# Second layer: first norm two batches ahead, the mixing's rows normed on VectorE, units evicted first

## The chip, the cores and the metric

One core of one Trainium2 chip runs the whole kernel. The metric is the device time of one execution in microseconds (us); lower is better. Five engines work from queues of their own and in order: TensorE (PE in the rows, PEld its weight loads), VectorE (DVE), ScalarE (ACT), GpSimd (POOL) and SyncE (SP, which only issues DMAs here). They wait for one another on semaphores.

## The reference, cut to what matters

x has 8 batches of 1024 tokens of 128 channels, in f32. Two layers follow each other; each adds an attention part and a feed-forward part to x, both behind a modulated norm. The change touches the second layer only (`B` is 8):

```python
h = layernorm(x) * (1 + ca) + sa            # the first norm
xn = h / max(norm(h), eps) * sqrt(128) * gamma
q, kv, a = split(xn @ W_qkva.T, 3); a = sigmoid(a)
y = scan over the tokens of y[t] = a[t] * y[t-1] + kv[t]
x = x + ga * q * y
h = layernorm(x) * (1 + cb) + sb            # the second norm, for the mixing
r = sigmoid((mu_r * h + (1 - mu_r) * h_prev) @ W_r.T)   # h_prev: h of the token before
k = (mu_k * h + (1 - mu_k) * h_prev) @ W_k.T
x = x + gb * r * (relu(k) ** 2 @ W_v.T)
```

## The kernel before, in words

The first layer (attention, then an expert layer with product keys) takes the time up to about 3208 us of the span; nothing of it changes. `build_second_layer` (L1109) is the rest. x2 holds x in SBUF, 128 tokens in the partitions, 8 tiles of 128x128 a batch. A batch goes through two halves of work: scanning (first norm, products, scan, addition to x2) and mixing (second norm, products, addition, store). The program is nine rounds, b = 0 to 8, written out in order for each engine. In round b the scanning of batch b and the mixing of batch b-1 run; the first norm of batch b+1 is made ahead in the same round. Semaphores tie the engines together; no loop of hardware and no planner is involved.

Within a round of before:

- TensorE turns the units of batch b (8 transposes, two PSUM banks `ring`), turns the normed rows of batch b-1 (8 transposes, banks `obank`), makes the products a, kv, q for both halves of 512 tokens (L1492, six products), then the k and r products of the mixing (L1509 to L1517) with the turns of y between them, the v products (L1522) and the turns of their gated result. Each matmul of a 512-column product stands in the rows as two f32 matmuls.
- ScalarE evicts the turned units into xnT (L1273), evicts the turned mixing rows into `shifted` (L1289), makes the decays (sigmoid of a, L1277), norms the rows of batch b+1 in one buffer `l1_h` (L1252, 8 activations), then the gates (relu L1294, sigmoid L1296, square L1298), the sums of squares of batch b+1 (L1260), its unit rows (L1266) and last the rows of the mixing of batch b (`mix_normed`, L1282, 8 activations). So the mixing rows stand in ScalarE's queue ahead of the next round's evictions.
- VectorE makes the first moments of batch b+1 (L1338, L1343, L1345), the shift (L1348), the scans (L1374, L1376), the scale and shift of h (L1362, L1365), the additions to x2 (L1380), the second moments, the floor of the norm (L1369), the second variance, the gated products (L1394), the second shift and the last additions (L1398).
- GpSimd makes the three roots of a round, each one `pow` of 128x8 values: of the first variance (L1219), of the norm (L1223), of the second variance (L1227).
- SyncE stores a half batch of x2 as soon as its mixing is added (L1212).

In PSUM, `ring` carries turned units, then a, then turned y; `obank` the turned mixing rows, then k and r, v, and the turned result.

Of the kernel before, what the change touches and what calls it, by code (L numbers as in the profile page):

```python
# [1108 lines left out]
def build_second_layer(nc, x2, c_sb, wmod, w_qkva, w_rkv, cols, ident, half_neg, ring, obank, wide, out):  # L1109
# [4 lines left out]
    with ExitStack() as ctx:  # L1114
# [18 lines left out]
        shift = sb("l1_shift", [P, 2, TB])  # L1133
# [3 lines left out]
        h = sb("l1_h", [P, TB, D])  # L1137
# [39 lines left out]
        shift2_ready = sem("l1_shift2")  # L1177
# [37 lines left out]
        @block.gpsimd  # L1215
        def _(pool):
            def first_rstd(b):
                pool.wait_ge(var1_ready, b + 1)
                nc.gpsimd.tensor_tensor(rstd[:, 0], var[:, 0], half_neg[:, 0:TB], ALU.pow).then_inc(rstd1_ready, 1)  # L1219

            def norm_root(b):
                pool.wait_ge(floored_ready, b + 1)
                nc.gpsimd.tensor_tensor(r_norm[:], floored[:], half_neg[:, 0:TB], ALU.pow).then_inc(r_norm_ready, 1)  # L1223

            def second_rstd(b):
                pool.wait_ge(var2_ready, b + 1)
                nc.gpsimd.tensor_tensor(rstd[:, 1], var[:, 1], half_neg[:, 0:TB], ALU.pow).then_inc(rstd2_ready, 1)  # L1227

            first_rstd(0)
            norm_root(0)  # L1230
            for b in range(B):
                if b + 1 < B:
                    first_rstd(b + 1)
                    norm_root(b + 1)
                second_rstd(b)

        @block.scalar
        def _(act):
# [10 lines left out]
            def normed(b):  # L1249
                act.wait_ge(shift1_ready, b + 1)  # L1250
                for t in range(TB):
                    last = nc.scalar.activation(h[:, t], x2[:, b * TB + t], ACT.Identity, bias=shift[:, 0, t:t + 1], scale=rstd[:, 0, t:t + 1])  # L1252
                last.then_inc(normed_ready, 1)

            def sums_of_squares(b):
                act.wait_ge(h_ready, b + 1)
                if b:
                    act.wait_ge(turned, 2 * b)
                for t in range(TB):
                    last = nc.scalar.activation(unit[:, t], h[:, t], ACT.Square, accum_out=squares[:, t:t + 1])  # L1260
                last.then_inc(squares_ready, 1)

            def unit_rows(b):
                act.wait_ge(r_norm_ready, b + 1)
                for t in range(TB):
                    made = nc.scalar.activation(unit[:, t], h[:, t], ACT.Copy, scale=r_norm[:, t:t + 1])  # L1266
                    if t % 4 == 3:
                        made.then_inc(unit_ready, 1)
# [9 lines left out]

            def mix_normed(b):
                act.wait_ge(shift2_ready, b + 1)  # L1280
                for t in range(TB):
                    made = nc.scalar.activation(mixed[:, t], x2[:, b * TB + t], ACT.Identity, bias=shift[:, 1, t:t + 1], scale=rstd[:, 1, t:t + 1])  # L1282
                    if t % 4 == 3:
                        made.then_inc(mixed_ready, 1)
# [17 lines left out]
            modulation_rows()  # L1302
            sums_of_squares(0)
            unit_rows(0)
            act.wait_ge(weights_ready, 5)
            for b in range(B + 1):
                scanning, mixing, ahead = b < B, b > 0, b + 1 < B
                if scanning:
                    turned_units(b)
                if mixing:  # L1310
                    shifted_h(b - 1)
                if scanning:
                    decays(b, 0)
                if ahead:
                    normed(b + 1)
                if scanning:
                    decays(b, 1)
                if mixing:
                    gates(b - 1, 0)
                if ahead:  # L1320
# [3 lines left out]
                if ahead:  # L1324
                    unit_rows(b + 1)
                if scanning:
                    mix_normed(b)

        @block.vector
        def _(dve):  # L1330
# [16 lines left out]
            def shift_of(which):  # L1347
                return nc.vector.scalar_tensor_tensor(shift[:, which], mean_var[:, which, :, 0], -1.0, rstd[:, which], ALU.mult, ALU.mult)  # L1348

# [6 lines left out]
            def first_shift(b):  # L1356
                dve.wait_ge(rstd1_ready, b + 1)
                shift_of(0).then_inc(shift1_ready, 1)

            def scaled(b):  # L1360
                dve.wait_ge(normed_ready, b + 1)
                link(nc.vector.scalar_tensor_tensor(h[:], row(1, b), 1.0, h[:], ALU.add, ALU.mult))  # L1362

            def moved(b):
                nc.vector.tensor_tensor(h[:], h[:], row(0, b), ALU.add).then_inc(h_ready, 1)  # L1365
# [16 lines left out]
            def second_moments(b):  # L1382
                dve.wait_ge(x_scanned, 2 * b + 2)
                if b:
                    dve.wait_ge(mixed_ready, 2 * b)
                moments_of(1, b)

            def second_shift(b):
                dve.wait_ge(rstd2_ready, b + 1)
                shift_of(1).then_inc(shift2_ready, 1)  # L1390
# [34 lines left out]
            modulation_cols()  # L1425
            dve.wait_ge(rows_ready, 4)
# [3 lines left out]
            for b in range(B + 1):  # L1430
                scanning, mixing, ahead = b < B, b > 0, b + 1 < B
                if ahead:
                    first_moments(b + 1)
                    first_shift(b + 1)
                if scanning:
                    scan(b, 0)
                if ahead:
                    scaled(b + 1)
                if scanning:
                    scan(b, 1)  # L1440
                if ahead:
# [5 lines left out]
                if ahead:  # L1447
                    floor_norm(b + 1)
                if scanning:
                    variance_of(1, var2_ready)  # L1450
# [3 lines left out]
                if scanning:  # L1454
                    second_shift(b)
                if mixing:
# [4 lines left out]
        def _(pe):  # L1461
# [69 lines left out]
            for b in range(B + 1):  # L1531
                scanning, mixing = b < B, b > 0
                if scanning:
                    turn_units(b)
                if mixing:
                    turn_mixed(b - 1)
                if scanning:
                    scan_products(b, 0)
# [101 lines left out]
```

## Time and profile before

| | us |
|---|---|
| median of 3 runs (3427.01 to 3428.05) | 3428.01 |
| the profiled execution's own time | 3427.62 |
| its span, first to last instruction | 3425.8 |
| second layer in it, from about 3208 | 218 |
| TensorE busy in the span | 3052.2 (89%) |
| VectorE busy | 2475.1 (72%) |
| ScalarE busy | 1380.5 (40%) |
| GpSimd busy | 165.3 (5%) |

The shares are averages over the whole kernel, most of which is the first layer. For the second layer, rows of single stretches are read: the windows by round, the chain of waits (followed back from the last instruction, printed in order of time), and the timelines of single engines (instructions in order of time, merged where alike, with the idle time before them in brackets). A group of equal short instructions overlaps in the pipe, so their pitch (from start to start) is below the duration of one.

### The profile page before, as it was taken

How to read it: one execution, taken by the hardware profiler on the slowest of the kernel's cores; microseconds unless marked ns; L12 is line 12 of the kernel's file. 1: busy time of each engine (PE TensorE's matmuls, PEld its weight loads, DVE VectorE, ACT ScalarE, POOL GpSimd, SP SyncE). 2: the span in 40 equal slices, each digit the busy share in tenths (PEclk: the TensorE clock that was granted, in tenths of full speed). 3: DMA queues.
4: the chain of work that ended last, by engine and by line, in shares of the span. 5: the costliest groups of instructions: out<-in, count | busy, mean ns of one | idle time of the engine just before them, and what ended most of it. 6: DMA issues, size and time to landing. Idle time of an engine off the chain costs nothing. (4 is left out here: it accounts for less than half of the span.)

```text
span 3425.8 us, 82744 instructions
## 1 busy us (share of the span) xinstructions
PE 3052.2 (89%) x32384; PEld 2451.8 (72%) x32384; DVE 2475.1 (72%) x8595; ACT 1380.5 (40%) x2532; POOL 165.3 (5%) x147
## 2 busy tenths in 40 slices
PE   5999999999999999999999965787888788877688
PEld 2888888888888888888888863555565555555443
DVE  4566665756766756756656556999999999999465
ACT  1544455544455544445544511222222222222476
POOL 0000000000000000000000000000000000000121
PEclk9999999999999999999999985767666766676699
DMA  1000000000000000000000011000000000000000
GB/s 67 1 1 7 1 1 8 1 1 8 1 1 8 1 1 7 1 2 7 1 7 1 1 48 59 0 0 0 0 0 0 0 0 0 0 0 1 1 22 28
DMA packets 7559, 25.35 MB, mean 7 GB/s; under 512 B 1472, under 2 KB 1984, under 8 KB 6976
## 3 DMA queue, kind: packets, MB, share of 16 engines
q1 hardware_dynamic: 7360, 22.57, 1.7%
q8 instruction: 140, 2.29, 0.3%
q14 instruction: 59, 0.48, 0.0%
HBM read 14.18 MB, written 8.39 MB: 7 GB/s over the span
## 5 line engine op out<-in xcount | busy, mean ns | idle before, releaser
L605 PEld LDWEIGHTS obank<-v_one,probs 128*128 128x128 f32 x8192 | 1069.2, 190 | 91.2 <-issue 2.3
L605 PE MATMUL obank<-v_one,probs 128*128 128x129 f32 x8192 | 1078.6, 274 | 0.0
L352 ACT ACTIVATE probs<-bank 128x512 f32<-128x512 f32 x1024 | 583.8, 597 | 747.3 <-PE bank L593 450.8
L442 DVE TENSOR_REDUCE maxes<-ring 128x1 f32<-128x512 f32 x1024 | 660.0, 687 | 128.4 <-PE ring L573 105.4
L592 PE MATMUL bank<-q_hh,k_hl 128*128 128x512 f32 x1024 | 505.3, 493 | 1.7 <-issue 1.5
L593 PE MATMUL bank<-q_lm,k_h 65*128 65x512 f32 x1024 | 406.5, 397 | 0.0
L455 DVE RECIPROCAL recip<-obank 128x1 f32<-128x1 f32 x512 | 83.9, 164 | 415.0 <-PE obank L605 401.1
L573 PE MATMUL ring<-k_hl,q_hh 128*128 128x512 f32 x1024 | 338.3, 410 | 10.5 <-DVE k_hl L434 6.0
L973 DVE TENSOR_TENSOR low_hot<-ids,low_iota 128x16384 f16<-128x16384 f16 x32 | 278.2, 8692 | 14.7 <-ACT ids L873 13.3
L573 PEld LDWEIGHTS ring<-k_hl,q_hh 128*128 128x128 f32 x1024 | 191.6, 191 | 83.4 <-DVE k_hl L434 25.7
L1048 PE MATMUL bank<-value_hot,low_hot 64*128 64x8 f16 x16384 | 216.8, 163 | 22.2 <-issue 15.3
L1048 PEld LDWEIGHTS bank<-value_hot,low_hot 64*128 64x128 f16 x16384 | 213.3, 96 | 27.1 <-issue 16.1
L592 PEld LDWEIGHTS bank<-q_hh,k_hl 128*128 128x128 f32 x1024 | 194.0, 189 | 19.8 <-issue 19.6
L593 PEld LDWEIGHTS bank<-q_lm,k_h 65*128 65x128 f32 x1024 | 196.7, 192 | 14.4 <-issue 13.9
L1029 PE MATMUL bank<-pk_hT,downT 128*128 128x256 f32 x512 | 187.8, 545 | 13.5 <-DVE z L995 13.5
L433 DVE TENSOR_TENSOR q_lm<-ring,q_hh 64x512 fp32r<-64x512 f32 x128 | 87.4, 682 | 147.1 <-ACT q_hh L330 147.1
L1029 PEld LDWEIGHTS bank<-pk_hT,downT 128*128 128x128 f32 x512 | 144.0, 289 | 56.4 <-DVE z L995 24.5
L1064 PE MATMUL ring<-up_gated,z 128*128 128x128 f32 x1024 | 169.9, 337 | 0.0
L460 DVE SCALAR_TENSOR_TENSOR acc<-obank,recip,acc 128x128 f32<-128x128 f32 x448 | 157.2, 351 | 15.9
L1064 PEld LDWEIGHTS ring<-up_gated,z 128*128 128x128 f32 x1024 | 167.0, 255 | 0.0
L928 DVE FIND_INDEX8 top_i<-top,sims 128x8 uint16<-128x32 f32 x1024 | 165.4, 184 | 0.0
L1062 PE MATMUL ring<-x,ident_sb 128*128 (+1 forms) x128 | 37.7, 388 | 136.7 <-DVE parts L979 135.3
(211 smaller groups left out, 3539.0 us busy)
## 6 DMA issues: line engine op xcount, KB each, us to landing
xt<-in_x SPq DMA_DIRECT2D x8, 512.0 KB, 8.7
out_x<-xt SPq DMA_DIRECT2D x8, 512.0 KB, 2.6
x<-out_x SPq DMA_DIRECT2D x1, 4096.0 KB, 12.0
out_x<-x SPq DMA_DIRECT2D x16, 256.0 KB, 2.1
pk_wq<-in_w_q SPq DMA_DIRECT2D x1, 1024.0 KB, 4.8
pk_wqT<-in_w_qT SPq DMA_DIRECT2D x1, 1024.0 KB, 6.8
wmod_sb<-in_wmod SPq DMA_DIRECT2D x2, 384.0 KB, 12.5
w_qk_sb<-in_w_qk SPq DMA_DIRECT2D x1, 512.0 KB, 4.4
```

The costliest lines, as they stand in the source:

```text
L352: nc.scalar.activation(probs[:, half, i, :], st[s % 4], ACT.Exp).then_inc(st_free[s % 4], 1)
L442: nc.vector.tensor_reduce(maxes[:, i, k:k + 1], ring[bank_of(at)][:], AX.X, ALU.max).then_inc(rows_maxed, 1)
L460: out = nc.vector.scalar_tensor_tensor(acc[:, tile, :], o[:, 0:D], recip[:, tile:tile + 1], acc[:, tile, :], ALU.mult, ALU.add)
L573: give(at, nc.tensor.matmul(bank[:], q_hh[s][:, i * P:(i + 1) * P], k_hl[s][:, k * HALF:(k + 1) * HALF], start=True, stop=True))
L592: nc.tensor.matmul(st[s % 4], k_hl[w][:, keys], q_hh[w][:, queries], start=True, stop=False)
L593: nc.tensor.matmul(st[s % 4], k_h1[w][:, keys], q_lm[w][:, queries], start=False, stop=True).then_inc(st_full[s % 4], 1)
L605: mm = nc.tensor.matmul(obank[j % 2][:, 0:D + 1], probs[:, half, m, cols], v_one[h % 2][:, m, :], start=(m == 0), stop=(m == TB - 1))
L928: nc.vector.max_index(top_i[:, s, q * H + h, :], top[:, s, q * H + h, :], sims[:, q, s, h, :])
L973: nc.vector.tensor_tensor(low_hot[:].rearrange("p t (m j) -> p t m j", j=2), spread(ids[:, 0], 2, P // 2), spread(low_iota[:].rearrange("p ...
L1029: mm = nc.tensor.matmul(wide[k][:, e * 2 * P:(e + 1) * 2 * P], downT[:, col:col + P], hT[:], start=True, stop=True)
L1048: mm = nc.tensor.matmul(wide[q][:, 8 * t:8 * t + 8], low_hot[rows, t, :], value_hot[rows, t, part, :], start=(part == 0), stop=(part == 1))
L1064: mm = nc.tensor.matmul(turn_bank[:, q * D:(q + 1) * D], z[:, e, q, :], up_gated[:, e, :], start=False, stop=(e == 7))
```

## The change

One norm buffer becomes two, and the first norm runs two batches ahead: moments, root, shift and normed rows of batch b+2 are made in round b, where those of b+1 were; before the loop, batches 0 and 1 are both normed. The scale, shift, sums of squares and unit rows of batch b+1 stay in round b. The rows of the mixing move from ScalarE (end of round b) to VectorE (start of round b+1) as 8 `tensor_scalar` instructions, (x - mean) * rstd, reading mean and rstd directly, so the second shift goes. In a round, ScalarE evicts both halves of the units first, then the first decay, then the turned mixing rows; TensorE puts the first half's products ahead of the turns of the mixing rows. On VectorE the scale and shift of h follow both scans, and the second variance stands ahead of the floor of the norm.

```diff
--- before.py
+++ after.py
-        shift = sb("l1_shift", [P, 2, TB])
+        shift = sb("l1_shift", [P, TB])
...
-        h = sb("l1_h", [P, TB, D])
+        h = [sb(f"l1_h{i}", [P, TB, D]) for i in range(2)]
...
@@ -1227,10 +1226,12 @@
                 nc.gpsimd.tensor_tensor(rstd[:, 1], var[:, 1], half_neg[:, 0:TB], ALU.pow).then_inc(rstd2_ready, 1)
 
             first_rstd(0)
+            first_rstd(1)
             norm_root(0)
             for b in range(B):
+                if b + 2 < B:
+                    first_rstd(b + 2)
                 if b + 1 < B:
-                    first_rstd(b + 1)
                     norm_root(b + 1)
                 second_rstd(b)
 
...
             def normed(b):
                 act.wait_ge(shift1_ready, b + 1)
                 for t in range(TB):
-                    last = nc.scalar.activation(h[:, t], x2[:, b * TB + t], ACT.Identity, bias=shift[:, 0, t:t + 1], scale=rstd[:, 0, t:t + 1])
+                    last = nc.scalar.activation(h[b % 2][:, t], x2[:, b * TB + t], ACT.Identity, bias=shift[:, t:t + 1], scale=rstd[:, 0, t:t + 1])
                 last.then_inc(normed_ready, 1)
...
-
-            def mix_normed(b):
-                act.wait_ge(shift2_ready, b + 1)
-                for t in range(TB):
-                    made = nc.scalar.activation(mixed[:, t], x2[:, b * TB + t], ACT.Identity, bias=shift[:, 1, t:t + 1], scale=rstd[:, 1, t:t + 1])
-                    if t % 4 == 3:
-                        made.then_inc(mixed_ready, 1)
...
@@ -1300,31 +1294,29 @@
             modulation()
             normed(0)
             modulation_rows()
+            normed(1)
             sums_of_squares(0)
             unit_rows(0)
             act.wait_ge(weights_ready, 5)
             for b in range(B + 1):
-                scanning, mixing, ahead = b < B, b > 0, b + 1 < B
+                scanning, mixing = b < B, b > 0
                 if scanning:
                     turned_units(b)
+                    decays(b, 0)
                 if mixing:
                     shifted_h(b - 1)
                 if scanning:
-                    decays(b, 0)
-                if ahead:
-                    normed(b + 1)
-                if scanning:
                     decays(b, 1)
+                if b + 2 < B:
+                    normed(b + 2)
                 if mixing:
                     gates(b - 1, 0)
-                if ahead:
+                if b + 1 < B:
                     sums_of_squares(b + 1)
                 if mixing:
                     gates(b - 1, 1)
-                if ahead:
+                if b + 1 < B:
                     unit_rows(b + 1)
-                if scanning:
-                    mix_normed(b)
...
-            def shift_of(which):
-                return nc.vector.scalar_tensor_tensor(shift[:, which], mean_var[:, which, :, 0], -1.0, rstd[:, which], ALU.mult, ALU.mult)
-
...
             def first_shift(b):
                 dve.wait_ge(rstd1_ready, b + 1)
-                shift_of(0).then_inc(shift1_ready, 1)
+                nc.vector.scalar_tensor_tensor(shift[:], mean_var[:, 0, :, 0], -1.0, rstd[:, 0], ALU.mult, ALU.mult).then_inc(shift1_ready, 1)
...
                 dve.wait_ge(x_scanned, 2 * b + 2)
+                moments_of(1, b)
+
+            def mix_normed(b):
+                dve.wait_ge(rstd2_ready, b + 1)
                 if b:
-                    dve.wait_ge(mixed_ready, 2 * b)
-                moments_of(1, b)
-
-            def second_shift(b):
-                dve.wait_ge(rstd2_ready, b + 1)
-                shift_of(1).then_inc(shift2_ready, 1)
+                    dve.wait_ge(mix_turned, 2 * b)
+                for t in range(TB):
+                    made = nc.vector.tensor_scalar(mixed[:, t], x2[:, b * TB + t], mean_var[:, 1, t, 0:1], rstd[:, 1, t:t + 1], ALU.subtract, ALU.mult)
+                    if t % 4 == 3:
+                        made.then_inc(mixed_ready, 1)
...
@@ -1423,37 +1415,37 @@
             weights()
             first_shift(0)
             modulation_cols()
+            first_moments(1)
+            first_shift(1)
             dve.wait_ge(rows_ready, 4)
             scaled(0)
             moved(0)
             floor_norm(0)
             for b in range(B + 1):
-                scanning, mixing, ahead = b < B, b > 0, b + 1 < B
-                if ahead:
-                    first_moments(b + 1)
-                    first_shift(b + 1)
+                scanning, mixing = b < B, b > 0
+                if mixing:
+                    mix_normed(b - 1)
+                if b + 2 < B:
+                    first_moments(b + 2)
                 if scanning:
                     scan(b, 0)
-                if ahead:
-                    scaled(b + 1)
+                if b + 2 < B:
+                    first_shift(b + 2)
                 if scanning:
                     scan(b, 1)
-                if ahead:
+                if b + 1 < B:
+                    scaled(b + 1)
                     moved(b + 1)
                 if scanning:
                     add_scanned(b, 0)
                     add_scanned(b, 1)
                     second_moments(b)
-                if ahead:
+                    variance_of(1, var2_ready)
+                if b + 1 < B:
                     floor_norm(b + 1)
-                if scanning:
-                    variance_of(1, var2_ready)
                 if mixing:
                     gated(b - 1, 0)
                     gated(b - 1, 1)
-                if scanning:
-                    second_shift(b)
-                if mixing:
                     add_mixed(b - 1, 0)
                     add_mixed(b - 1, 1)
...
@@ -1532,10 +1524,10 @@
                 scanning, mixing = b < B, b > 0
                 if scanning:
                     turn_units(b)
+                    scan_products(b, 0)
                 if mixing:
                     turn_mixed(b - 1)
                 if scanning:
-                    scan_products(b, 0)
                     scan_products(b, 1)
                 if mixing:
                     k_product(b - 1, 0)
```

The semaphore of the second shift goes with it, and the other users of `h` read and write `h[b % 2]`.

## Rows read from the trace of the kernel before

**Rows 1.** Windows by round: length, busy time and count per engine, granted clock (PEclk), DMA.
```profile
3224.82:3243.28 18.46, 10.57 (x28) 5.35 (x28) 10.81 (x36) 10.54 (x37) 3.31 (x3) 0.68 0.00 0
3243.28:3267.06 23.78, 21.12 (x59) 10.48 (x60) 13.83 (x47) 17.79 (x52) 4.87 (x4) 0.80 0.01 1
...
3314.35:3336.31 21.96, 18.95 (x67) 9.12 (x66) 15.47 (x50) 17.73 (x53) 4.88 (x4) 1.00 0.06 24
3336.31:3359.66 23.35, 20.32 (x67) 9.97 (x66) 15.57 (x50) 17.79 (x52) 4.87 (x4) 0.93 0.06 24
...
3383.19:3425.80 42.61, 33.06 (x108) 15.71 (x106) 15.28 (x36) 20.68 (x44) 3.21 (x2) 0.96 0.10 37
```

**Rows 2.** Chain of waits, the round from 3314.35 to 3336.31: start, us, what.
```profile
3314.35 2.45 ACT l_unit L1266 x8
3316.80 3.09 ACT l_mixed L1282 x8
...
3320.59 1.04 PE ring L1492 x2
...
3323.35 0.86 PE ring L1492 x2
...
3331.51 0.45 PE ring L1464 x4
...
3331.99 0.70 DVE x L1380
...
3334.39 0.18 DVE l_floored L1369
...
3334.64 1.65 POOL l_r_norm L1223
```

**Rows 3.** Timeline of TensorE: turned units, v product, next products; end of round 7.
```profile
3316.86 0.66 PE L1464 MATMUL ring<-ident_sb,l_unit 128*128 128x128 f32 x4 [0.51 <-ACT l_unit L1266]
...
3334.97 1.10 PE L1522 MATMUL obank<-kact,w_rkv 128*128 128x512 f32 x2 [0.41 <-ACT kact L1298]
...
3342.79 1.91 PE L1492 MATMUL ring<-xnT,w_qkva 128*128 128x512 f32 x2
...
3405.50 1.10 PE L1522 MATMUL obank<-kact,w_rkv 128*128 128x512 f32 x2 [0.44 <-ACT kact L1298]
...
3411.63 1.12 PE L1509 MATMUL obank<-shifted,w_now 128*128 128x512 f32 x2
```

**Rows 4.** Timeline of ScalarE: opening, a full round, the last mixing rows.
```profile
3212.70 3.19 ACT L1252 ACTIVATE l_h<-x,l_shift,l_rstd 128x128 f32<-128x128 f32 x8 [1.66 <-DVE l_shift L1348]
...
3220.42 0.31 ACT L1260 ACTIVATE l_unit<-l_h 128x128 f32<-128x128 f32 x1 [2.61 <-DVE l_h L1365]
...
3227.43 0.69 ACT L1273 ACTIVATE xnT<-ring,l_gamma 128x512 f32<-128x512 f32 x1 [0.17 <-PE ring L1464]
...
3319.79 1.24 ACT L1273 ACTIVATE xnT<-ring,l_gamma 128x512 f32<-128x512 f32 x2
...
3407.72 3.19 ACT L1282 ACTIVATE l_mixed<-x,l_shift,l_rstd 128x128 f32<-128x128 f32 x8 [2.37 <-DVE l_shift L1348]
```

**Rows 5.** Timeline of VectorE: opening, round 0, one full round.
```profile
3217.90 1.23 DVE L1362 SCALAR_TENSOR_TENSOR l_h<-l_mod_rows,l_h 128x1024 f32<-128x1024 f32 x1 [4.09 <-ACT l_mod_rows L1247]
...
3238.36 1.28 DVE L1380 TENSOR_TENSOR x<-x,ring 128x512 f32<-128x512 f32 x2
...
3312.51 0.64 DVE L1343 BATCH_NORM_AGGREGATE l_mean_var<-l_moments 128x2 f32<-128x6 f32 x8
3313.18 0.17 DVE L1345 TENSOR_SCALAR l_var<-l_mean_var 128x8 f32<-128x8 f32 x1
```

**Rows 6.** Timeline of VectorE: single-source operations on 128x128 tiles elsewhere.
```profile
3210.70 0.47 DVE L1404 TENSOR_SCALAR w_now<-w_rkv,cols 128x128 f32<-128x128 f32 x2
...
3134.59 0.23 DVE L963 TENSOR_SCALAR chosen_u<-chosen_u 128x128 uint32<-128x128 uint32 x1
3134.73 0.22 DVE L965 TENSOR_SCALAR chosen_u<-chosen_u 128x128 uint32<-128x128 uint32 x1
```

More of the change, by code:

```diff
@@ L1176, in build_second_layer @@
         rstd2_ready = sem("l1_rstd2")
-        shift2_ready = sem("l1_shift2")
         mixed_ready = sem("l1_mixed_ready")
@@ L1259, in sums_of_squares @@
                 for t in range(TB):
-                    last = nc.scalar.activation(unit[:, t], h[:, t], ACT.Square, accum_out=squares[:, t:t + 1])
+                    last = nc.scalar.activation(unit[:, t], h[b % 2][:, t], ACT.Square, accum_out=squares[:, t:t + 1])
                 last.then_inc(squares_ready, 1)
@@ L1265, in unit_rows @@
                 for t in range(TB):
-                    made = nc.scalar.activation(unit[:, t], h[:, t], ACT.Copy, scale=r_norm[:, t:t + 1])
+                    made = nc.scalar.activation(unit[:, t], h[b % 2][:, t], ACT.Copy, scale=r_norm[:, t:t + 1])
                     if t % 4 == 3:
@@ L1357, in first_shift @@
                 dve.wait_ge(rstd1_ready, b + 1)
-                shift_of(0).then_inc(shift1_ready, 1)
+                nc.vector.scalar_tensor_tensor(shift[:], mean_var[:, 0, :, 0], -1.0, rstd[:, 0], ALU.mult, ALU.mult).then_inc(shift1_ready, 1)
             def scaled(b):
                 dve.wait_ge(normed_ready, b + 1)
-                link(nc.vector.scalar_tensor_tensor(h[:], row(1, b), 1.0, h[:], ALU.add, ALU.mult))
+                link(nc.vector.scalar_tensor_tensor(h[b % 2][:], row(1, b), 1.0, h[b % 2][:], ALU.add, ALU.mult))
             def moved(b):
-                nc.vector.tensor_tensor(h[:], h[:], row(0, b), ALU.add).then_inc(h_ready, 1)
+                nc.vector.tensor_tensor(h[b % 2][:], h[b % 2][:], row(0, b), ALU.add).then_inc(h_ready, 1)
             def floor_norm(b):
```

## The prediction

> **What bounds the kernel now.** I read the page first (TensorE busy 89% of the span), then windows cut at each start of the unit rows (L1266), since the shares are averages and the change touches only the last 218 us. A round of the second layer takes 21.96 us where TensorE has its full clock throughout (PEclk 1.00, 2.4 GHz), and 23.35 where part of it runs at 1.2 GHz (0.93) [rows 1]; three more rounds, not shown, are of the second kind, at 23.5 to 23.7. In all of them TensorE, the busiest engine, has 19 to 21 us of work, VectorE 15.5, ScalarE 17.8. So none is full, and the order of the work decides. The chain of waits shows it for the round from 3314.35 [rows 2]: ScalarE makes the unit rows (2.45), then the mixing rows (3.09); only then are the units evicted, and the products start at 3320.59, 6.24 us after the round's start. From there TensorE is busy without a gap until the second turn of y ends at 3331.96 (11.37). VectorE adds it to x2 at 3331.99, takes the second moments and floors the norm at 3334.39, GpSimd makes the root (1.65), and the next unit rows start at 3336.31 (4.32 after the addition). 6.24 + 11.37 + 0.03 + 4.32 = 21.96. The reader is to see that ScalarE's mixing rows (3.09) stand in the chain between the unit rows and their own eviction.
>
> **The part that pays: evictions at once.** The last units are turned 2.51 after the round's start and take 0.66 [rows 3], so both banks are full at 3.17. ScalarE evicts them together from 5.44 to 6.68 (3319.79, 1.24 for two) [rows 4]. With the mixing rows out of its queue it is free at 2.45, evicts the first half by 2.45 + 0.69 = 3.14, and the first product starts at 3.15. The opening batch already does this: its first eviction starts 2.61 after its unit rows [rows 4]. Gain 6.24 - 3.15 = 3.09 a round.
>
> **What comes back.** (1) The two turns of the mixing rows stood beside ScalarE's work and now stand between the first and second half's products, in TensorE's gapless stretch: 2 x 0.45 by the turn of y [rows 2] = 0.90. They hold nothing else up: with three products of 0.86 a half [rows 2], turn 0 ends near 6.2, ScalarE makes `shifted` by 7.7, and the k product is due at 9.2. (2) The second variance now stands ahead of the floor: 0.67 for the aggregation until its successor, 0.08 for the addition [rows 5] = 0.75, on the path, since it lies between moments and root. New round at full clock: 3.15 + 11.37 + 0.90 + 0.03 + 4.32 + 0.75 = 20.52, against 21.96: 1.44 less.
>
> **The mixing rows on VectorE.** 8 `tensor_scalar` of 128x128 f32 from SBUF with two scalars per partition. The nearest row, the same operation with one such scalar (w_now), takes 0.47 for two at 0.28 each, a pitch of 0.19 [rows 6]; integer ones with constants have a pitch of 0.14 [rows 6]; the upper bound is ScalarE's 3.09 / 8 = 0.39 [rows 2]. I take 0.19, 8 x 0.19 + 0.09 = 1.6 us (bounds 1.2 and 3.2). They wait for the second root, which GpSimd makes after the norm's, 1.65 after the round's start; so they stand from 1.7 to 3.3, and the moments and variance of b+2 follow (1.7 + 0.75), the first scan near 5.7. The turns want the rows at 5.8; y is wanted by TensorE at 12.6 and ready, about 2 later than the scan's start, at 7.8. VectorE's second use, scale and shift of h (2.5) after both scans, ends near 13.0, before the first addition at 13.2. Cover is thus 2.5 us for the rows; the path feels them through first shift and ScalarE's normed rows only above that (below). In the round the edit costs nothing; VectorE's work goes from 15.5 to some 17 of 20.5. Removing the second shift gives 0.08 of VectorE, off the path. The Trainium skill, "VectorE: DVE Perf Modes", the section "The perf-mode tier table", says that an f32 `tensor_scalar` from SBUF to SBUF runs at two elements a cycle. The w_now row (0.28, against 0.23 of the integer row of the same size) does not agree for the form with a scalar per partition; by the rule the rows would take about the lower bound, which moves only the tail, by 0.2.
>
> **ScalarE's new order.** Its total falls by 3.1. The normed rows of b+2 (3.19 by batch 0's [rows 4]) run from 8.2 to 11.3, after the second decay; the first relu is wanted at 11.0 and made by 11.9, the second k product wants it at 13.0 (after the turn of y). Slack 1.1. Two batches ahead nothing waits for these rows in the same round; GpSimd's first root is asked for at 5.8 and ready at 7.5, in an otherwise idle stretch. The stores on SyncE keep their order and come with the last additions.
>
> **Opening and round 0.** The second batch's norm now stands ahead of the first one's scale. Normed rows of batch 0 end at 3212.70 + 3.19 = 3215.89 [rows 4]; then moments 1.7, variance 0.75, root 1.65, shift: 3220.2, and scale and shift of h, 1.23 each, which began at 3217.90 [rows 5], end at 3222.7. ScalarE makes the second batch's rows (3.19) until 3223.4 and only then the sums of squares that began at 3220.42 [rows 4]: 2.9 later. Round 0 took 18.46 [rows 1]; in it the additions began at 3238.36, 13.5 after its start [rows 5]. With both scans ahead of scale and shift, VectorE gets h done at about 14.4 and adds then: 0.9, and the variance 0.7: 1.6 longer. Together +4.5.
>
> **Rounds 1 to 6** took 139.9 (3243.28 to 3383.19) [rows 1]. New: 6 x 20.52 = 123.1, plus 1.8 for the low clock after round 0's idle time (23.78 - 21.96, kept), = 124.9.
>
> **The clock.** A round at 0.93 costs 1.4 (1.7 in the rounds not shown) more than one at 1.00 [rows 1]; the low stretch begins with the first products. Ahead of it TensorE has, from the second v product's end (3334.97 + 1.10) to the products (3342.79), 6.7 us of nothing but turns and gaps [rows 3]. In the tail the same kind of stretch is 3406.60 to 3411.63, 5.0 us [rows 3], with no fall. After the change it is about 4.4 (19.1 to 23.6 in a round's time). So the clock should mostly hold. I put one fall of 1.7 into rounds 2 to 7 where there were five; bounds none and six (0 to 10.2). Rounds 1 to 6: 126.6 with it, a gain of 13.3.
>
> **The tail**, from 3383.19 to the end, 42.6 [rows 1] with one fall: -1.7; products earlier, turns between, -3.09 + 0.90 = -2.2 (the variance already stood there); the last mixing rows on VectorE: they started on ScalarE at 3407.72 [rows 4] and the k product at 3411.63 [rows 3], 3.9 later. On VectorE, by the same clock, 1.1 until the last additions are through, 0.85 for four rows, 0.7 turn, 0.7 `shifted` = 3.3, so -0.6. Gain 4.5, 2.8 if the clock falls.
>
> **The sum**, on the profiled execution: span 3425.8 + 4.5 - 13.3 - 4.5 = 3412.5; its own time lies 1.8 above its span, so 3414.3, and 0.4 more for the median of the runs (3428.01 against 3427.62): 3414 to 3415. I say 3414.
>
> **Rivals.** (1) The clock falls in every round, as in five of six before. The turns-only stretch of 4.4 lies close to the tail's 5.0, one instance, and round-to-round idle is still there; against it, 6.7 shrinks by a third. Five falls more, 5 x 1.7 = 8.5: 3423, within 0.2%. (2) The mixing rows on VectorE cost far more than their row. They delay moments, first shift, ScalarE's normed rows, relu, and so the second k product. It decides from 1.6 + 1.1 = 2.7 us for the eight on; at 0.65 each (5.2) each of seven rounds loses 2.5 and the tail 3.6: +21, 3435, slower. For: two scalars per partition, a form with no row; against: even ScalarE has 0.39, where the loss is 0.5 a round (+5). (3) The early start is given back: the wait moves from the unit rows to VectorE, whose queue is now the one with h, both scans and the rows in it; with only 0.7 of the 1.44 gained a round, in six rounds and the tail, 7 x 0.7 = 4.9: 3419. For: h is through 0.2 before the first addition; against: the second addition, which counts, is 2 later.
>
> **Chances.** Forecast (at most two falls, 3410 to 3418) 0.70; rival 1, 0.12; rival 3, 0.09; rival 2, 0.04; better than 3410, 0.05 (opening cheaper). A measurement of this kernel tells about 0.2%, 6.9 us, from no change, so faster means under 3421.2: 0.86; same 0.10; slower 0.04. The range runs from 3409 to 3422: below, no fall at all and half of the opening's cost hidden; above, nearly all falls.
>
> **What would show it.** In the windows of the new kernel a period of 20.5 at PEclk 1.00; in the timeline xnT evicted at 2.45 and products at 3.15 after the unit rows; in the chain no mixing rows, but the variance between moments and root; the rows on VectorE at a pitch near 0.19 from 1.7 on; the start of the first unit rows 2.9 later. It is wrong if the chain of a round passes through ScalarE's normed rows or relu, if PEclk stays at 0.93 in most rounds, or if round 0 grows by over 3.

## The result, and the profile after

The changed kernel takes 3409.73 us (median of 5 runs, 3407.49 to 3412.46) against 3427.15 (5 runs, 3426.11 to 3428.05): a ratio of 0.995, interval 0.9938 to 0.9963. Forecast were 3414, range 3409 to 3422.

The profiled execution took 3412.22 with a span of 3410.3, 15.5 less than before. Not all of it belongs to the change. The second layer's first instruction, ScalarE's table load, stands at 3206.28 here and at 3208.08 in the trace of before; over all profiles of this study, whose first 3200 us are the same code, it stands anywhere from 3205.7 to 3210.0. So I compare the layer from that table load to the end of the span: 217.7 us before, 204.0 after, 13.7 less. The predicted sum was 13.3 less.

The windows by round, as in [rows 1], cut at the starts of the unit rows (L1267 is L1266 of before):

```profile
3226.13:3246.39 20.26, 10.65 (x28) 5.38 (x28) 10.79 (x36) 10.53 (x36) 3.30 (x3) 0.67 0.00 0
3246.39:3267.73 21.34, 19.27 (x61) 9.82 (x62) 16.35 (x55) 14.94 (x44) 4.87 (x4) 0.89 0.00 1
...
3308.72:3329.22 20.50, 18.49 (x65) 9.14 (x65) 17.43 (x57) 14.82 (x44) 4.87 (x4) 1.00 0.07 26
...
3370.22:3410.30 40.08, 31.86 (x104) 15.51 (x103) 18.56 (x49) 14.64 (x28) 3.21 (x2) 0.96 0.11 40
```

Five rounds, from 3267.73 on, take 20.50 us each (the first 20.49) at PEclk 1.00, where one of before did at 21.96 and the others took 23.4 to 23.7 [rows 1]. VectorE is busy for 17.4 of them, ScalarE for 14.8; in the last of the five, which norms no further batch, for 15.1 and 11.9. The chain of waits of the same round as in [rows 2]:

```profile
3308.72 2.45 ACT l_unit L1267 x8
...
3311.88 1.04 PE ring L1484 x2
...
3314.64 0.87 PE obank L1456 x8
...
3324.15 0.70 DVE x L1369
...
3324.87 1.66 DVE l_moments L1330 x8
...
3326.55 0.65 DVE l_mean_var L1335 x8
...
3327.23 0.17 DVE l_var L1337
...
3327.55 1.65 POOL l_r_norm L1222
```

The mixing rows are gone from it. From the unit rows' start to the first product: 3.16 (6.24 in [rows 2]). The eight turns of the mixing rows stand between the products (0.87), and the second variance between moments and root (0.65 + 0.17, less the overlap). On ScalarE's timeline, opening and one round:

```profile
3218.66 3.19 ACT L1253 ACTIVATE l_h<-x,l_shift,l_rstd 128x128 f32<-128x128 f32 x8 [2.66 <-DVE l_shift L1347]
3221.76 0.29 ACT L1261 ACTIVATE l_unit<-l_h 128x128 f32<-128x128 f32 x1
...
3311.08 0.67 ACT L1274 ACTIVATE xnT<-ring,l_gamma 128x512 f32<-128x512 f32 x1
...
3316.93 3.18 ACT L1253 ACTIVATE l_h<-x,l_shift,l_rstd 128x128 f32<-128x128 f32 x8
3320.02 0.57 ACT L1288 ACTIVATE kact<-obank 128x512 f32<-128x512 f32 x1
```

The second batch's normed rows keep the sums of squares waiting until 3221.76 (batch 0 of before [rows 4]: 3220.42, in a layer that began 1.8 later), so the first unit rows start 19.85 after the layer's start where they started after 16.74. In the round the first eviction starts 2.36 after the unit rows, normed rows two batches ahead follow, and the relu is not late.

### The profile page after: what moved, and what is told of

It is laid out like the page before. It is cut to its first block and busy times, and to the rows that moved or that the text cites. A ratio compares the mean times of both kernels' runs of the same rounds, so it can differ in the third digit from the quotient of the medians.

```text
span 3410.3 us, 82730 instructions
## 1 busy us (share of the span) xinstructions
PE 3040.3 (89%) x32384; PEld 2448.4 (72%) x32384; DVE 2488.9 (73%) x8651; ACT 1355.8 (40%) x2468; POOL 165.3 (5%) x147
## 5 line engine op out<-in xcount | busy, mean ns | idle before, releaser
L973 DVE TENSOR_TENSOR low_hot<-ids,low_iota 128x16384 f16<-128x16384 f16 x32 | 278.1, 8691 | 14.1 <-ACT ids L873 13.1
L1048 PE MATMUL bank<-value_hot,low_hot 64*128 64x8 f16 x16384 | 216.9, 163 | 23.4 <-issue 16.1
L1029 PE MATMUL bank<-pk_hT,downT 128*128 128x256 f32 x512 | 188.1, 546 | 13.7 <-DVE z L995 13.5
```

Of the source, the lines that this page charges most:

```text
L973: nc.vector.tensor_tensor(low_hot[:].rearrange("p t (m j) -> p t m j", j=2), spread(ids[:, 0], 2, P // 2), spread(low_iota[:].rearrange("p ...
L1029: mm = nc.tensor.matmul(wide[k][:, e * 2 * P:(e + 1) * 2 * P], downT[:, col:col + P], hT[:], start=True, stop=True)
L1048: mm = nc.tensor.matmul(wide[q][:, 8 * t:8 * t + 8], low_hot[rows, t, :], value_hot[rows, t, part, :], start=(part == 0), stop=(part == 1))
```

## The experiments

Each is read by its layer time (from ScalarE's table load to the end of the span, in one profiled execution) and its rounds; the ratios are against the kernel before, run on the same chip. In all, the code of the first 3200 us is unchanged. Full rounds of one kernel repeat within 0.1 (the exceptions are named), but with the same instructions the tail has come out 1.6 apart and rounds 0 and 1 together 0.7 apart (both below), and most intervals of the ratios overlap. So layer times less than about 2 apart say nothing by themselves.

| kernel | layer, us | full round, us | median, us | ratio (interval) |
|---|---|---|---|---|
| before | 217.7 | 21.96 to 23.7 | 3427 to 3430 | 1 |
| the change | 204.0 | 20.50 | 3409.73 | 0.995 (0.9938 to 0.9963) |
| 1 floor ahead of the variance | 198.9 | 19.75 | 3407.01 | 0.9935 (0.9919 to 0.9952) |
| 2 mixing rows back on ScalarE | 225.5 | 23.9 to 24.2 | 3433.71 | 1.0019 (1.001 to 1.0028) |
| 3 mixing rows on VectorE alone | 204.6 | 21.54 (first 20.93) | 3413.59 | 0.9956 (0.994 to 0.9973) |
| 4 opening in another order | 201.4 | 20.50 | 3409.42 | 0.9944 (0.9928 to 0.9961) |
| 5 before, turns made thrice | 210.0 | 21.96 | 3418.81 | 0.9975 (0.9964 to 0.9985) |
| 6 extra row instructions | 207.2 | 20.84 (last 20.50) | 3415.68 | 0.9964 (0.9951 to 0.9977) |
| 7 mixing rows turned first | 204.8 | 20.74 | 3412.99 | 0.9957 (0.994 to 0.9974) |
| 8 floor ahead of the moments | 191.2 | 19.14 | 3399.63 | 0.9921 (0.9907 to 0.9935) |
| 9 gated products ahead too | 197.6 | 20.2 (last 19.23) | 3407.90 | 0.9937 (0.992 to 0.9953) |
| 10 wide row instructions | 204.9 | 20.7 (last 20.50) | 3413.81 (one run) | none |

**1. The floor of the norm ahead of the second variance**, on VectorE of the changed kernel:

```diff
                     second_moments(b)
-                    variance_of(1, var2_ready)
                 if b + 1 < B:
                     floor_norm(b + 1)
+                if scanning:
+                    variance_of(1, var2_ready)
```

> The changed kernel with one order put back on VectorE: the floor of the norm ahead of the second variance. My theory, that the variance (0.64 + 0.17) stands on the path between moments and root: a round falls from 20.50 to 19.75, rounds 1 to 6 by 4.5, round 0 by 0.75, the tail not at all, in sum 5 us: 3405, the layer 199 us from its table load on where the changed kernel has 204. Rival, that the second root, which GpSimd now gets later than the norm's and the mixing rows wait for, takes the place: the mixing rows start at the same 1.6 after the unit rows, since GpSimd makes the roots in the same order, so nothing should be given back; if it is, a round stays near 20.5 and the time near 3410.

A window of one round and the chain:

```profile
3290.07:3309.82 19.75, 18.48 (x67) 9.14 (x66) 17.35 (x57) 14.96 (x44) 4.87 (x4) 1.00 0.08 28
```

```profile
3327.65 0.18 DVE l_floored L1358
...
3327.90 1.65 POOL l_r_norm L1222
```

The floor follows the moments again and a round is 0.75 shorter, the layer 5.1, as my theory had it. That one order of the change cost 5 us of the layer: 3.75 in five full rounds, 1.1 in rounds 0 and 1, 0.25 in the tail.

**2. The mixing rows back on ScalarE**, at the end of the round, with the second shift on VectorE and TensorE's turns ahead of the products as before (both not shown); two batches ahead and the variance ahead of the floor stay:

```diff
                 if b + 1 < B:
                     unit_rows(b + 1)
+                if scanning:
+                    mix_normed(b)
...
```

> The changed kernel with the mixing rows back on ScalarE at the end of a round, with their shift, and TensorE's turns of them ahead of the products as before; two batches ahead, the order of VectorE and the first decay ahead of the turned rows stay. Theory (the gain comes from the rows leaving ScalarE's queue ahead of the evictions; two batches ahead alone buys nothing): products again start 6.2 us after the unit rows, the variance ahead of the floor costs 0.75, so a round takes 22.7 at full clock and 24.4 where it falls, opening and round 0 cost 5: the layer 225 to 233 us against 217.7 before, 3435 to 3441. Rival (two batches ahead is what pays): a round at or under 21.96, the layer under 218, 3428 or less.

```profile
3318.49:3342.49 24.00, 20.23 (x65) 9.96 (x65) 15.48 (x49) 17.80 (x53) 4.87 (x4) 0.93 0.06 22
```

ScalarE's timeline of that round:

```profile
3320.84 3.17 ACT L1285 ACTIVATE l_mixed<-x,l_shiftb,l_rstd 128x128 f32<-128x128 f32 x8
3323.91 1.24 ACT L1276 ACTIVATE xnT<-ring,l_gamma 128x512 f32<-128x512 f32 x2
```

The mixing rows stand ahead of the evictions again, which start 5.42 after the unit rows. The low clock is back (0.93), a round takes 24.0, and the kernel is slower than before by 0.2%. Of the 7.8 us by which the layer is longer, 3.1 are the opening and some 5 are the variance ahead of the floor (experiment 1), so the norm two batches ahead wins next to nothing in the rounds while the mixing rows stay on ScalarE.

**3. The mixing rows on VectorE alone**, in the kernel before:

```diff
                 scanning, mixing, ahead = b < B, b > 0, b + 1 < B
+                if mixing:
+                    mix_normed(b - 1)
                 if ahead:
                     first_moments(b + 1)
...
```

`mix_normed` is VectorE's of the change; ScalarE's and the second shift go.

> The kernel before with one part of the change alone: the rows of the mixing on VectorE at the start of the next round; first norm one batch ahead, all other orders old. Theory A (what pays is only that the mixing rows leave the way from unit rows to eviction): products start about 4.25 after the unit rows instead of 6.24, VectorE makes the first shift at about 8.0, both scans are through at 14.4, and a round takes about 20.6, the same as in the changed kernel, without the 5 us that opening and round 0 cost there: layer about 200 us, 3405. Theory B (the two batches ahead are needed): first moments, root and shift of the next batch now stand behind the mixing rows and ahead of the scans, ScalarE's normed rows come at 8.0 to 11.1, scale and shift of h and the sums of squares end after the second moments, and the round takes 21.5 or more: 3412 or more.

```profile
3305.62:3327.15 21.53, 18.57 (x65) 9.11 (x64) 17.35 (x57) 15.06 (x44) 4.86 (x4) 1.00 0.07 25
```

The chain of that round:

```profile
3312.78 1.65 POOL l_rstd L1218
...
3314.65 3.19 ACT l_h L1251 x8
...
3317.87 1.24 DVE l_h L1352
...
3319.13 1.29 DVE scanned L1364
```

Theory B held for the round: rows, first root (1.65), ScalarE's normed rows (3.19), scale of h and second scan now lie in one line, and the round takes 21.54, as B had it (21.5 or more; 3412 or more, against 3413.59). That is 1.04 more than in the change. The layer is 204.6, which can't be told from the change's 204.0. But this kernel keeps the floor ahead of the variance, and the change doesn't. The fair partner is experiment 1, where the floor is ahead too: its round is 1.79 shorter and its layer 5.7, though its opening is 3.1 longer. At most 0.24 a round of that is TensorE's order (experiment 7); the rest is the first norm two batches ahead, with the orders on VectorE and ScalarE that go with it; no run parts these.

**4. The opening in another order**, changed kernel:

```diff
             first_moments(1)
-            first_shift(1)
             dve.wait_ge(rows_ready, 4)
             scaled(0)
             moved(0)
+            first_shift(1)
...
-            normed(1)
             sums_of_squares(0)
+            normed(1)
```

> The changed kernel with only its opening in another order: VectorE scales and shifts h of batch 0 ahead of the second batch's shift, ScalarE makes the first sums of squares ahead of the second batch's normed rows. Theory: the opening up to the first unit rows, 19.85 us in the changed kernel against 16.74 before, is on the path and costs by ScalarE's normed rows (3.19) standing ahead of the sums; now root (1.65) and normed rows (3.1) overlap, the unit rows start 1.5 us earlier and everything follows: 1.5 us less, 3408. Rival: what is won there is lost in round 0, because VectorE's moments of batch 2 wait for those normed rows: no change, 3410.

The tail:

```profile
3369.02:3407.50 38.48, 30.25 (x104) 14.82 (x103) 18.56 (x49) 14.65 (x28) 3.20 (x2) 1.00 0.11 42
```

The first unit rows start 18.30 after the layer's start, 1.55 earlier. Rounds 0 and 1 take 42.1 together (41.6 in the change), so 1.0 of it stays, in two traces whose rounds 0 and 1 can move by 0.7 without any edit. The other 1.6 of the layer's gain is the tail: 38.48 at PEclk 1.00 against 40.08 at 0.96, which the edit does not touch. The whole-kernel times don't resolve it.

**5. The kernel before with turns made three times**, the second half of the units and the first half of the mixing rows, in TensorE's gaps:

```diff
+                    for again in range(2 * k):
+                        turn(ring[k], lambda i: unit[:, 4 * k + i])
                     turn(ring[k], lambda i: unit[:, 4 * k + i]).then_inc(turned, 1)
...
+                    for again in range(2 * (1 - k)):
+                        turn(obank[k], lambda i: mixed[:, 4 * k + i])
                     turn(obank[k], lambda i: mixed[:, 4 * k + i]).then_inc(mix_turned, 1)
```

> The kernel before, with two groups of turns made three times over on TensorE, results the same: the second half of the units and the first half of the mixing rows. The extra turns lie in TensorE's gaps between the v products and the next products, where the evictions are waited for anyway, so at the same clock nothing moves. Theory (the low clock at the start of the products comes from TensorE having only turns and gaps in the 6.7 us before them, and is a cost apart from the waits): the clock stays at 1.00 in most of the rounds 2 to 7, five of them go from 23.5 to 21.96, the layer from 217.7 to about 210, 3420. Rival (turns do not hold the clock, whatever their number): rounds stay near 23.5, 3427.

```profile
3266.91:3288.87 21.96, 20.69 (x83) 10.87 (x82) 15.46 (x50) 17.73 (x52) 4.87 (x4) 1.00 0.06 24
```

With more work and no wait removed, rounds 2 to 6 all take 21.96 at PEclk 1.00 and the layer is 7.7 us shorter: 6.3 in rounds 2 to 6, 1.5 in the tail (PEclk 0.98). So the low clock was a cost of its own, and this much of it could be had back.

**6. Extra row instructions** ahead of the mixing rows in the changed kernel:

```diff
+                for t in range(4):
+                    nc.vector.tensor_scalar(spare[:, t], x2[:, b * TB + t], rstd[:, 1, t:t + 1], None, ALU.mult)
+                for t in range(4, TB):
+                    nc.vector.tensor_scalar(spare[:, t], x2[:, b * TB + t], 0.5, 2.0, ALU.subtract, ALU.mult)
```

> The changed kernel with eight more row instructions on VectorE ahead of the mixing rows, into a tile that nobody reads: four with one scalar per partition, four with constants. It doubles the suspected cost of my second rival and measures the pitch of the three forms (the rows of the change: 0.26 to 0.27 with two scalars). Extra 1.2 to 2.1 us a round. Theory: the slack up to the point where TensorE waits for the relu is 1.3 us in the changed kernel's trace (relu ready 3320.6, k product 3321.96), so a round grows by the excess, 0 to 0.8 us, to 20.5 to 21.3, and the tail by the whole 1.2 to 2.1: 3411 to 3417. Rival (VectorE is now the bound): each round grows by all of it, 20.5 to 22.1 or more, 3420 and above.

A window of one round, and the place in its chain where TensorE now waits for the relu ("issue"):

```profile
3310.57:3331.41 20.84, 18.72 (x65) 9.20 (x65) 18.58 (x65) 14.84 (x44) 4.87 (x4) 1.00 0.07 26
```

```profile
3323.81 0.10 issue
3323.91 1.10 PE obank L1506 x2
```

The mixing rows start 1.33 us later and the round grows by 0.34: about 1.0 is slack, and VectorE at 18.6 of 20.84 is not the bound. The durations by form (one scalar per partition, constants, and the change's rows with two scalars), min/median/max in ns:

```profile
L1381 DVE TENSOR_SCALAR l_spare<-x,l_rstd x32: 279/282/289, 3248.2 to 3395.0; 128x128 f32<-128x128 f32 x32
L1383 DVE TENSOR_SCALAR l_spare<-x x32: 219/222/225, 3249.0 to 3395.6; 128x128 f32<-128x128 f32 x32
...
L1385 DVE TENSOR_SCALAR l_mixed<-x,l_mean_var,l_rstd x64: 337/344/347, 3249.6 to 3397.5; 128x128 f32<-128x128 f32 x64
```

**7. Both turns of the mixing rows ahead of all products**, changed kernel:

```diff
                     turn_units(b)
-                    scan_products(b, 0)
                 if mixing:
                     turn_mixed(b - 1)
                 if scanning:
+                    scan_products(b, 0)
                     scan_products(b, 1)
```

> The changed kernel with TensorE's old order: both turns of the mixing rows ahead of both halves' products. Theory: the rows are ready 3.75 after the unit rows on VectorE, so the second turn ends at 4.25 and the products start then instead of at 3.16 plus 0.87 for the turns in between: 0.2 us a round more, 1.5 us in sum, 3411, so the new order on TensorE is worth little. Rival 1 (units first is what pays): products start later by the rows' whole time, 1.1 us a round, 7 us in sum, 3417. Rival 2: with the turns there again the stretch without products grows and the clock falls in most rounds, 1.6 us each: 3421.

A full round:

```profile
3308.05:3328.79 20.74, 18.52 (x65) 9.13 (x65) 17.52 (x57) 14.83 (x44) 4.87 (x4) 1.00 0.07 26
```

0.24 a round, and the clock holds. TensorE's new order is worth hardly anything.

**8. The version to beat both**: experiment 4's opening, and

```diff
                     add_scanned(b, 1)
-                    second_moments(b)
-                    variance_of(1, var2_ready)
                 if b + 1 < B:
                     floor_norm(b + 1)
+                if scanning:
+                    second_moments(b)
+                    variance_of(1, var2_ready)
```

> The version to beat both: the changed kernel with the opening of the fourth experiment, and the floor of the norm ahead of the second moments too, not only of the second variance. Theory: of VectorE's 3.2 us between the second addition and the floor all but about 0.3 (the squares come 0.3 after the addition) leave the path, 2.2 a round against the changed kernel; TensorE's own work of 18.5 us and its wait for the gates then bound the round at 18.6 to 19.1; six rounds give 9 us, opening 1.5, round 0 up to 1: the layer 192 to 194 against 204, 3398 to 3401. Rival (the second norm takes the place: its moments, variance and root come 0.3 later, relative to the unit rows 1.8 later, so the mixing rows, first shift and relu delay the k product): a round at 19.7 or more, no better than the floor ahead of the variance alone, 3405.

```profile
3300.91:3320.05 19.14, 18.18 (x64) 9.16 (x64) 17.23 (x58) 14.94 (x45) 4.91 (x3) 1.00 0.08 28
```

The end of the chain of this round:

```profile
3318.30 1.56 DVE l_moments L1330 x8
...
3320.56 0.17 DVE l_var L1337
3320.73 1.38 DVE rgate L1386 x2
...
3322.15 0.66 PE obank L1457 x4
3322.81 0.45 PE ring L1457 x4
...
3323.28 0.70 ACT xnT L1274
```

The best of the study: 0.9921 of the kernel before, 10 us under the change by the medians of two series and 12.8 in the layer. My theory held for the size (a round of 18.6 to 19.1, measured 19.14; a layer of 192 to 194, measured 191.2), not for what bounds the round. I had TensorE's work and its wait for the gates; the chain still runs through moments and variance, no longer to the root but to the gated products and their turns, behind which the units' second turn is queued on TensorE.

**9. The gated products ahead of the variance**, on top of 8:

```diff
                     second_moments(b)
-                    variance_of(1, var2_ready)
                 if mixing:
                     gated(b - 1, 0)
                     gated(b - 1, 1)
+                if scanning:
+                    variance_of(1, var2_ready)
```

> The version with the floor ahead of the second moments, and on VectorE the gated products ahead of the second variance. Theory: there the chain goes from the moments over the variance (0.75) to the gated products and TensorE's turns of them, behind which the second turn of the units is queued; with the variance behind, these turns come 0.75 earlier and a round falls from 19.14 to 18.5 to 18.7, near TensorE's own 18.2 of work; the layer 188 us, 3396. Rival: the second root comes 1.5 us later, the mixing rows start at 3.9 instead of 3.4 after the unit rows, first shift and relu follow, and TensorE waits there instead: a round at 19.1 or more, 3400.

```profile
3304.37:3324.58 20.21, 18.20 (x64) 9.34 (x64) 17.17 (x57) 14.73 (x45) 4.91 (x3) 1.00 0.07 26
```

```profile
3315.42 0.17 DVE l_shift L1347
...
3315.61 3.19 ACT l_h L1253 x8
3318.80 0.49 ACT kact L1288
...
3319.42 1.10 PE obank L1504 x2
```

The rival was right in what takes over, and far too low in its price (3400, against 3407.90): the second gated product waits for its v product, the variance stands behind it, and the mixing rows start 4.64 after the unit rows, against 3.40 in experiment 8, where the rival had 3.9. So first shift, ScalarE's normed rows (3.19) and relu keep the k product until 3319.42, and the round takes 20.2. The later second root used up the slack that experiment 6 had measured.

**10. Wide row instructions**, three extra ones of 128x512 a round in the changed kernel, for their durations only:

```diff
+                nc.vector.tensor_scalar(spare[:, 0], x2[:, some(b, 0)], rstd[:, 1, 0:1], None, ALU.mult)
+                nc.vector.tensor_scalar(spare[:, 1], x2[:, some(b, 0)], mean_var[:, 1, 0, 0:1], rstd[:, 1, 0:1], ALU.subtract, ALU.mult)
+                nc.vector.tensor_scalar(spare[:, 2], x2[:, some(b, 0)], 0.5, 2.0, ALU.subtract, ALU.mult)
```

> The changed kernel with three extra VectorE instructions a round ahead of the mixing rows, each of 128x512 f32 from SBUF into a tile that nobody reads: with one scalar per partition, with two, with constants. It is for their durations only. At 128x128 the three forms took 282, 342 and 222 ns. If scalars per partition only add a fixed part (about 60 ns each) and every form goes at two elements a cycle, 384 columns more add 0.20 us: about 480, 540 and 420 ns. If the forms with such scalars go at one element a cycle, they add 0.40 us: 680 and 740 beside 420.

```profile
L1380 DVE TENSOR_SCALAR l_spare<-x,l_rstd x8: 480/486/489, 3247.1 to 3392.7; 128x512 f32<-128x512 f32 x8
L1381 DVE TENSOR_SCALAR l_spare<-x,l_mean_var,l_rstd x8: 537/542/543, 3247.5 to 3393.1; 128x512 f32<-128x512 f32 x8
L1382 DVE TENSOR_SCALAR l_spare<-x x8: 417/421/422, 3248.0 to 3393.6; 128x512 f32<-128x512 f32 x8
```

384 columns more cost 0.20 us in every form (282 to 486, 344 to 542, 222 to 421 ns), 1.9 columns a ns each time, and each scalar per partition adds some 60 ns at either width. With the clock of 0.96 GHz that the Trainium skill's page "VectorE: DVE Perf Modes" gives under "Specifications", that is, as an estimate, two elements a cycle.

## Why the prediction was right, point by point

| term | predicted, us | measured, us |
|---|---|---|
| first product after the unit rows, a round | 3.15 | 3.16 |
| turns of the mixing rows on the path | 0.90 | 0.87 |
| second variance on the path | 0.75 | 0.75 (experiment 1) |
| full round | 20.52 | 20.50 |
| opening | +2.9 | +3.1 |
| round 0 | +1.6 | +1.8 |
| rounds 1 to 6 | -13.3 | -16.1 |
| tail | -4.5 | -2.5 |
| layer | -13.3 | -13.7 |

- **Evictions at once, turns and variance** are shown: the chain of the change has them at their predicted lengths, experiment 1 isolates the variance, experiment 2 the mixing rows' place, experiment 7 TensorE's order.
- **The clock** was mis-sized in both directions. I put one fall of 1.7 into rounds 2 to 7; none came in rounds 2 to 6 (1.7), and round 1 lost 0.8 instead of 1.8 (1.0): together the 2.8 by which rounds 1 to 6 are better. The tail kept the fall that I took out of it, at another place. There TensorE's stretch of turns before the last k product is 5.0 us long, from 3388.63 + 1.10 on:

```profile
3388.63 1.10 PE L1514 MATMUL obank<-kact,w_rkv 128*128 128x512 f32 x2 [0.44 <-ACT kact L1292]
...
3394.69 1.94 PE L1501 MATMUL obank<-shifted,w_now 128*128 128x512 f32 x2
3396.43 1.71 PE L1502 MATMUL obank<-shifted,w_prev 128*128 128x512 f32 x2
```

The first two pairs take 1.94 and 1.71. In the tail of before a stretch of the same length had passed without a fall [rows 3], and in experiment 4 the same turns with the same waits did:

```profile
3387.43 1.10 PE L1514 MATMUL obank<-kact,w_rkv 128*128 128x512 f32 x2 [0.44 <-ACT kact L1292]
...
3393.35 1.13 PE L1501 MATMUL obank<-shifted,w_now 128*128 128x512 f32 x2
```

Over all profiles, the tail with these turns stands at 0.96 in the change and in experiments 1, 3 and 7, and at 1.00 in 4 and 8. The same stretch goes both ways, and my reading of a single instance as a safe bound was wrong, if only by 1.6 us. In the rounds the stretch is 4.1 us (I had 4.4), and there no fall was seen. The tail's other 0.4 is the mixing rows: from the last v product to the k product I took 0.6 off, and at full clock it is 5.92 (experiment 4) after 6.13 [rows 3]. That the clock gate made part of the gain is shown by experiment 5; 7.7 us of the layer could be had from it alone, and the order of the work is worth about 210.0 - 204.0 = 6.0 beyond that (the tails still differ a little in clock, 0.98 and 0.96).
- **Round 0** grew as forecast in this trace (20.26 at PEclk 0.67, before 18.46 at 0.68). But in experiments 2, 6, 7 and 10, with the same instructions up to there, it took 18.6 to 18.8 at 0.77, and in 6, 7 and 10 round 1 then took 22.2 to 22.3 instead of 21.34. When the clock rises in the opening rounds I had taken as given; it moves 0.9 us between two rounds and 0.7 in their sum. So the growth of 1.6 is confirmed at one clock history only, and this trace could have shown much less of it in round 0.
- **The mixing rows on VectorE** take

```profile
3310.33 2.14 DVE L1380 TENSOR_SCALAR l_mixed<-x,l_mean_var,l_rstd 128x128 f32<-128x128 f32 x8 [0.38 <-POOL l_rstd L1226]
```

2.14 for eight, where I took 1.6 from w_now's pitch (0.19); inside my bounds of 1.2 to 3.2, and hidden in the rounds as forecast. I had set the row against the rule of the Trainium skill, "VectorE: DVE Perf Modes", the section "The perf-mode tier table" (f32 `tensor_scalar` in SBUF at two elements a cycle), and believed the row. Experiment 10 shows that the rule holds with scalars per partition too; what made w_now longer than the integer row was the scalar's fixed 60 ns, and I had one size only, from which a slope cannot be told.
- **The rivals.** The clock fell at the products of none of the rounds 2 to 6 (rival 1). Rows too dear to hide (rival 2): experiments 6 and 9 show the mechanism where I placed it, relu behind the normed rows, with 1.0 us of slack (1.1 predicted). Nothing was given back in the rounds (rival 3).
- **Luck in the number.** The layer's 13.3 meets 13.7 because errors cancel: rounds 1 to 6 came out 2.8 better, the tail 2.0 worse, opening and round 0 together 0.4 worse. And 3409.73 lies just below the 3410 to 3418 that I gave 0.70, in the band that I gave 0.05 and explained by a cheaper opening; the opening was dearer. The profiled execution, forecast at 3414.3, took 3412.22, 1.8 of the difference being the layer's earlier start; the median lies another 2.5 lower.
- **Not settled:** the medians fell by 17.4 us, the layer of the two profiles by 13.7. Where the other 3.7 lie is not shown: the code ahead of the layer is the same, but its length differs by up to 4 us between profiles, and the layer of the executions without a profile is not known.

What the prediction did not ask is what each part of the change is worth. By layer times, the mixing rows on VectorE alone give 217.7 - 204.6 = 13.1; two batches ahead without them give next to nothing (experiment 2, less the variance's 5); both together, with the floor in its old place, give 217.7 - 198.9 = 18.8. So the first norm two batches ahead, with the orders that go with it, pays 5.7 us on top of the other part, opening included, and the order of variance and floor (5.1) took nearly all of that away again.

## What to carry to other kernels

Look in the chain for an instruction that stands in an engine's queue between a producer and the eviction of its own result, and move that one first; then check every step of the new order that lies between the last operand and the root that starts the next round, as one small operation (0.75 us) ahead of it costs as much as a third of the gain. Running a stage further ahead lengthens the opening once and shortens each round, but only when what stood in front of it is out of the way: here 5.7 us of a layer with the mixing rows moved, next to nothing without. When a change has several parts, take each out alone, and compare kernels that differ in that part only. Where TensorE waits with only short work in its queue, part of the time can be its low clock, and repetitions of harmless work in its gaps show how much.

## What the runs showed of the hardware

- Repeated turns (transposes through TensorE) in otherwise idle gaps kept the granted clock at 1.00 in rounds 2 to 6; without them it fell to 1.2 GHz at the start of the products in four of these five. The layer took 7.7 us less (experiment 5).
- One and the same stretch of turns and waits in the tail (4.8 us at full clock) ended at 1.2 GHz in some traces (the change, experiments 1, 3 and 7) and at 2.4 GHz in others (4 and 8).
- On VectorE a `tensor_scalar` of 128x128 f32 in SBUF takes 222 ns with constants, 282 with one scalar per partition, 344 with two; at 128x512 421, 486 and 542 (experiments 6 and 10).
